# Attention in a decoder layer: row sums collected by four accumulating DMAs and used two chunks later

## What is computed

```python
qkv = jnp.einsum('bnd,ed->bne', x, w_qkv)
q, k, v = jnp.split(qkv, 3, axis=-1)          # to heads: (2, 16, 2048, 32)
dots = jnp.einsum('bhnd,bhmd->bhnm', q, k) * SCALE
attn = jax.nn.softmax(dots, axis=-1)
out = jnp.einsum('bhnm,bhmd->bhnd', attn, v)
...
x = _layernorm(x + attention)                 # then cross-attention to 77 rows, and a quantised FFN
```

## Time and profile before

| | us |
|---|---|
| median of 3 runs (lowest, highest) | 1822.68 (1819.03, 1823.56) |
| profiled execution, own time | 1825.24 |
| its span, first to last instruction | 1823.4 |
| busy TensorE, VectorE, ScalarE, GpSimd | 1770.6, 1450.9, 1445.7, 194.8 |
| mean TensorE clock granted | 0.989 of full speed |
| self-attention, first exponential to end of the last | 294.12 to about 1347.8 |

### The profile page before, as it was taken

How to read it: one execution, slowest core, us unless ns; L and a number is a source line. 1 busy time by engine, 2 the same in 40 slices (tenths; PEclk the granted TensorE clock), 3 DMA queues, 4 the chain that set the end, 5 groups by cost and what they waited for, 6 DMA issues and landing times. The chain is left out here.

```text
span 1823.4 us, 40231 instructions
## 1 busy us (share of the span) xinstructions
PE 1770.6 (97%) x15938; PEld 900.4 (49%) x15938; DVE 1450.9 (80%) x1582; ACT 1445.7 (79%) x1581; POOL 194.8 (11%) x189
## 2 busy tenths in 40 slices
PE   8999999999999999999999999999989999999997
PEld 6887885333333333333333333333346776644443
DVE  5345345988998898899998999989984778788898
ACT  5344356999999999999999999999964555555487
POOL 0000000010010010010010010010112221000044
PEclk9999999999999999999999999999999999999999
DMA  8665556658567577477566667676556340122075
GB/s 295 212 236 205 199 204 198 139 123 191 128 142 180 120 160 174 114 164 177 128 150 169 146 148 177 136 179 149 117 143 212 139 138 24 64 127 127 1 293 209
DMA packets 110832, 288.79 MB, mean 158 GB/s; under 512 B 8676, under 2 KB 25188, under 8 KB 97252
## 3 DMA queue, kind: packets, MB, share of 16 engines
q1 hardware_dynamic: 97012, 187.08, 28.7%
q0 software_dynamic: 13680, 99.62, 28.4%
HBM read 105.01 MB, written 82.05 MB: 103 GB/s over the span
## 5 line engine op out<-in xcount | busy, mean ns | idle before, releaser
L918 DVE TENSOR_TENSOR dve_sum<-dve_sum,probs 128x2048 f32<-128x2048 f32 x320 | 733.6, 2292 | 34.3 <-ACT probs L842 25.6
L842 ACT ACTIVATE probs<-score_others,shift_now 128x1536 f32<-128x1536 f32 x384 | 597.4, 1556 | 0.0
L1035 PE MATMUL mixed_ps<-probs,value_piece 128*32 128x512 f32 (+1 forms) x3840 | 402.9, 516 | 1.1 <-ACT probs L842 0.2
L841 ACT ACTIVATE probs<-score_first,shift_now 128x512 f32<-128x512 f32 x384 | 267.0, 695 | 2.2 <-PE score_others L997 1.1
L997 PE MATMUL score_first<-first_queries,key_piece 32*128 32x512 f32 x768 | 248.3, 429 | 4.3 <-ACT probs_paired L841 1.9
L997 PE MATMUL score_others<-first_queries,key_piece 32*128 32x512 f32 x2304 | 251.0, 429 | 0.0
L997 PE MATMUL score_others<-q_second,key_piece 32*128 32x512 f32 x2304 | 247.4, 424 | 0.0
L997 PE MATMUL score_first<-q_second,key_piece 32*128 32x512 f32 x768 | 245.1, 424 | 0.1
L997 PEld LDWEIGHTS score_first<-first_queries,key_piece 32*128 32x128 f32 x768 | 123.2, 185 | 186.0 <-ACT probs L841 94.9
L997 PEld LDWEIGHTS score_first<-q_second,key_piece 32*128 32x128 f32 x768 | 121.8, 183 | 183.4 <-ACT probs L841 105.4
L842 ACT ACTIVATE probs_paired<-score_others,shift_now 128x1536 f32<-128x1536 f32 x128 | 202.4, 1581 | 0.0
(11 more groups left out here) (253 smaller groups left out, 2581.7 us busy)
## 6 DMA issues: line engine op xcount, KB each, us to landing
probs_paired<-probs_paired POOLq DMA_DIRECT2D x95, 1024.0 KB, 8.4
o_scratch<-out_parts SPq DMA_DIRECT2D x33, 512.0 KB, 2.8
k_scratch<-parts SPq DMA_DIRECT2D x32, 512.0 KB, 4.6
q_scratch<-parts SPq DMA_DIRECT2D x32, 512.0 KB, 2.7
key_piece<-k_scratch SPq DMA_DIRECT2D x32, 512.0 KB, 5.1
h_scratch<-h SPq DMA_DIRECT2D x5, 2816.0 KB, 8.1
h<-h_scratch SPq DMA_DIRECT2D x5, 2816.0 KB, 11.5
v_scratch<-values SPq DMA_DIRECT2D x32, 256.0 KB, 2.0
```

The lines of the kernel that those rows point to most:

```text
L841: nc.scalar.activation(block_probs(k)[:, 0:CH], score_first[:], ACT.Exp, bias=shift[:, c:c + 1], scale=SCALE).then_inc(probs_done, 1)
L842: nc.scalar.activation(block_probs(k)[:, CH:HPG * CH], score_others[n % 2][:], ACT.Exp, bias=shift[:, c:c + 1], scale=SCALE).then_inc(prob ...
L918: nc.vector.tensor_tensor(total[:], first[:], block_probs(k)[:], ALU.add).then_inc(dve_added, 1)
L1035: last = nc.tensor.matmul(mixed_ps[j * HD:(j + 1) * HD, lo:hi], v_group[k // KPP][:, k % KPP, j * HD:(j + 1) * HD], block_probs(k)[:, j * ...
```

## The change

The pairs become late blocks, (8, 9) and (13, 14). `join_pair` adds block 9 onto 8 and 14 onto 13; `join_sum` then adds each joined pair onto `dve_sum` by a further DMA, the first after VectorE's last add of the chunk, the second after the first has landed. `dve_sum` then holds the sum of all 16 blocks, and TensorE needs one pass of sums a chunk, in step 0, on the chunk before the last one (BEHIND = 2). The results of a chunk wait in one of two buffers `mixed` meanwhile. Value products begin in step 1, with two steps of three halves instead of four. VectorE's copy of the results stands after the last add instead of before it. ScalarE waits for `pair_free` before each block of a pair, which GpSimd raises when a pair's sum has landed. SP's wait for `four_landed` goes. At the end the last two chunks' sums are made on their own: `sums_last_but_one` in step 14 of the last chunk, `sums_last` in five passes.

```diff
-    PAIRS = ((2, 3), (4, 5))
+    PAIRS = ((8, 9), (13, 14))
...
-    SUM_PARTS = 2
-    SUMS_AT = ((0,), (1,))
+    BEHIND = 2
+    CHUNKS = ITERS * CPB
...
-    VALUE_HALVES = (0, 0, 2, 2, 3, 2, 2, 3, 2, 2, 3, 2, 2, 3, 2, 2)
+    VALUE_HALVES = (0, 2, 2, 2, 2, 3, 2, 2, 2, 2, 3, 2, 2, 2, 2, 2)
...
-        mixed = sb("mixed", [P, CH], F32)
+        mixed = [sb(f"mixed{u}", [P, CH], F32) for u in range(BEHIND)]
...
-                            sp.wait_ge(four_landed, 1 + (it + 1) * CPB)
-                            values_read(0)
-                            load_v(ng, nb, 0)
-                            keys_read(2)
...
+                            for piece in range(PIECES):
+                                values_read(piece)
+                                load_v(ng, nb, piece)
+                                if piece + 2 < PIECES:
+                                    keys_read(piece + 2)
+                                    load_k(ng, nb, piece + 2)
...
-                            if i is not None and k == PAIRS[i][1]:
-                                act.wait_ge(pairs_landed, it * CPB + c + 1)
-                            elif i == 0:
-                                act.wait_ge(four_landed, it * CPB + c + 1)
-                            elif i == 1:
-                                act.wait_ge(sums_done, it * CPB + c + 2)
+                            if i is not None:
+                                act.wait_ge(pair_free, 2 * (it * CPB + c) + 1 + i)
...
+                def add(it, c, a):
+                    k = ADD_ORDER[a + 1]
+                    total = dve_sum[c % 2]
+                    v.wait_ge(probs_done, (it + 1) * EXPS + (c * KB + k + 1) * 2)
+                    if a == 0:
+
+                        v.wait_ge(sums_done, 2 + it * CPB + c)
+                        first = block_probs(ADD_ORDER[0])
+                    else:
+                        v.wait_ge(dve_added, (it * CPB + c + 1) * ADDS + a)
+                        first = total
+                    nc.vector.tensor_tensor(total[:], first[:], block_probs(k)[:], ALU.add).then_inc(dve_added, 1)
+
+                def chunk(it, c, adds):
+                    take_shift(it if c == 0 else it + 1, (c + CPB - 1) % CPB)
+                    invert(it * CPB + c)
+                    divide(it * CPB + c, c)
+                    for a in range(adds):
+                        add(it, c, a)
+
+                with v.Fori(0, ITERS - 1) as it:
                     for c in range(CPB):
...
+                        chunk(it, c, ADDS)
+                        gather(it, c + 1)
+                for c in range(CPB - 1):
+                    chunk(ITERS - 1, c, ADDS)
+                    gather(ITERS - 1, c + 1)
+                chunk(ITERS - 1, CPB - 1, ADDS - 1)
+                invert(CHUNKS, last_but_one_ps)
+                gather(ITERS - 1, CPB)
+                divide(CHUNKS, 0)
+                invert(CHUNKS + 1)
...
+                def join_pair(it, c, i):
+                    into, other = PAIRS[i]
+
+                    pool.wait_ge(mixed_done, (it + 1) * BLOCKS + c * KB + into + 1)
+                    pool.wait_ge(probs_done, (it + 1) * EXPS + (c * KB + other + 1) * 2)
+                    pool.sem_inc(may_join, 1)
+                    nc.gpsimd.dma_start(probs_paired[i][0][:], probs_paired[i][1][:], accum_op=ALU.add).then_inc(pair_joined[i], 16)
+
+                def join_sum(it, c, i):
+                    f = it * CPB + c
+                    pool.wait_ge(pair_joined[i], 16 * (f + 1))
+                    if i == 0:
+                        pool.wait_ge(dve_added, (f + 2) * ADDS)
+                    pool.sem_inc(may_join, 1)
+                    nc.gpsimd.dma_start(dve_sum[c % 2][:], probs_paired[i][0][:], accum_op=ALU.add).then_inc(sum_joined, 16)
+                    pool.wait_ge(sum_joined, 32 * f + 16 * (i + 1))
+                    pool.sem_inc(pair_free, 1)
+
                 def join(it, c):
...
+                    for i in range(len(PAIRS)):
+                        join_pair(it, c, i)
+                    for i in range(len(PAIRS)):
+                        join_sum(it, c, i)
...
+                def sums(f):
+                    pe.wait_ge(mixed_copied, f + BEHIND)
                     if f == 0:
...
+                        pe.sem_inc(sums_done, 1)
+                    elif f < BEHIND:
+                        fill().then_inc(sums_done, 1)
                     else:
...
+                        pe.wait_ge(sum_joined, 32 * (f - 1))
+                        ones_times(mixed_ps, dve_sum[f % 2], True, True).then_inc(sums_done, 1)
+
+                def sums_last_but_one():
+                    pe.wait_ge(probs_done, EXPS + (CHUNKS * KB - 1) * 2)
+                    pe.wait_ge(sum_joined, 32 * (CHUNKS - 1))
+                    ones_times(last_but_one_ps, dve_sum[CHUNKS % 2], True, True).then_inc(sums_done, 1)
+
+                def sums_last():
+                    pe.wait_ge(mixed_copied, CHUNKS + BEHIND)
+                    pe.wait_ge(probs_done, EXPS + CHUNKS * KB * 2)
+                    raw = [*PAIRS[1], ADD_ORDER[-1]]
+                    pe.wait_ge(pair_joined[0], 16 * CHUNKS)
+                    ones_times(mixed_ps, probs_paired[0][0], True, False)
+                    for k in raw:
+                        ones_times(mixed_ps, block_probs(k), False, False)
+                    pe.wait_ge(dve_added, (CHUNKS + 1) * ADDS - 1)
+                    ones_times(mixed_ps, dve_sum[(CHUNKS - 1) % 2], False, True).then_inc(sums_done, 1)
...
-                        for at in SUMS_AT[step] if step < len(SUMS_AT) else ():
-                            sums(f, at)
+                        if step == 0:
+                            sums(f)
+                        if f == CHUNKS - 1 and step == KB - AHEAD:
+                            sums_last_but_one()
```

More of the change, by code:

```diff
@@ L699, in attend @@
         dve_added, may_join = sem("dve_added"), sem("may_join")
-        pair_joined, four_joined = sem("pair_joined"), sem("four_joined")
-        pairs_landed, four_landed = sem("pairs_landed"), sem("four_landed")
+        pair_joined, sum_joined = [sem(f"pair_joined{i}") for i in range(len(PAIRS))], sem("sum_joined")
+        pair_free = sem("pair_free")
         mixed_copied = sem("mixed_copied")
@@ L815, in _ @@
                     sp.wait_ge(v_in[piece], 16 * ITERS)
-                store(ITERS, 0)
+                for c in range(BEHIND):
+                    store(ITERS, c)
             @block.scalar
@@ L896, in _ @@
                 v.wait_ge(filled, 1)
-                gather(0, 0)
-                with v.Fori(0, ITERS) as it:
-                    for c in range(CPB):
[L900 to L904, removed]
-                        for a in range(ADDS):
-                            if a == ADDS - 1:
-                                gather(it, c + 1)
-                            k = ADD_ORDER[a + 1]
-                            v.wait_ge(probs_done, (it + 1) * EXPS + (c * KB + k + 1) * 2)
-                            if a == 0:
-                                v.wait_ge(sums_done, 1 + it * CPB + c)
-                                first = block_probs(ADD_ORDER[0])
-                            else:
-                                v.wait_ge(dve_added, (it * CPB + c + 1) * ADDS + a)
-                                first = total
-                            nc.vector.tensor_tensor(total[:], first[:], block_probs(k)[:], ALU.add).then_inc(dve_added, 1)
@@ L999, in score, with ones_times @@
                     last.then_inc(scores_done, 1)
-                def sums(f, at, parts=SUM_PARTS):
-                    if at == 0:
-                        pe.wait_ge(mixed_copied, f + 1)
-                    if f == 0:
-                        if at == 0:
-                            pe.sem_inc(sums_done, 1)
-                        return
-                    if f == CHUNKS and at < len(PAIRS):
-                        part = probs_paired[at][0]
-                        pe.wait_ge(pair_joined, 16 * len(PAIRS) * CHUNKS)
-                    elif at == 0:
-                        part = probs_paired[1][0]
-                        pe.wait_ge(four_joined, 16 * f)
-                    else:
-                        part = dve_sum[(f + 1) % 2]
-                        pe.wait_ge(dve_added, (f + 1) * ADDS)
-                    for j in range(HPG):
-                        last = nc.tensor.matmul(mixed_ps[j * HD:(j + 1) * HD, :], keep.ones[:, 0:HD], part[:, j * CH:(j + 1) * CH],
-                                                start=at == 0, stop=at == parts - 1)
-                    if at == parts - 1:
-                        last.then_inc(sums_done, 1)
+                def ones_times(out, part, start, stop):
+                    for j in range(HPG):
+                        last = nc.tensor.matmul(out[j * HD:(j + 1) * HD, :], keep.ones[:, 0:HD], part[:, j * CH:(j + 1) * CH],
+                                                start=start, stop=stop)
+                    return last
```

(20 more changed lines are left out.)

64 lines of the change are left out of this document (22 added, 42 removed).

## The result

The changed kernel takes 1834.72 us (median of 5 runs, 1829.54 to 1839.56) and the kernel before 1820.06 (5 runs, 1819.03 to 1823.56): a ratio of 1.0068, 95% interval 1.0044 to 1.0092, so slower by 14.7 us where the forecast was slower by 39.6. The direction is that of the forecast and the time lies in its whole range (1805 to 1882), just under the forecast's own part of it (1836 to 1882), but the loss is less than half of what was forecast.

What follows compares the result with a forecast made beforehand. ScalarE's exponentials set the pace in two-half steps, TensorE in three-half ones. Terms -7.0 - 9.0 + 0.8 + 44.8 + 10.0 = +39.6 us on a median of 1822.7 gave 1862; range 1805 to 1882, the forecast's own 1836 to 1882.

Steps and rivals of the forecast that it cites:

- The term of -7.0: Ordinary attention chunks: two three-half TensorE steps fewer gain 0.22 us in each of 32 chunks, -7.0 us.
- Rival (c): Block 6: VectorE's first add comes too late and VectorE sets the pace, 1825 us without chain stands; chance 0.02.
- -9.0: ScalarE's four waits for POOL's joined blocks, with restarts and half-clock losses, go: -9.0 us.
- +44.8: Block 8, first chunk of an iteration: ScalarE stands 6.4 us for POOL's late accumulations, seven times, +44.8 us.
- my 9.0: POOL's chain, fourth chunk: the second sum takes 7.8 us plus 1.2 for key and value loads.
- The bound below: Lower bound of ScalarE's stand at block 8, from cheaper split and accumulations: 2.3 us, or none if loads slip into gaps.
- +10.0: TensorE after each of the seven ScalarE stands: the clock falls and loses 1.43 us each time, +10.0 us.
- +0.8: End of attention: extra inversion and five passes of last sums, less one add, +0.8 us (bounds -1.5 and +3).
- my 4.2: POOL's split of the weights, fourth chunk: takes 4.2 us amid back-to-back VectorE adds (range 3.3 to 5.7).
- Rival (b): POOL's chain is late by 1 to 3 us only, about +4 us, 1826 us; chance 0.07.
- (a): POOL's chain fits because accumulations and loads overlap more; only the gains of -15.2 us remain, 1807 us; chance 0.22.
- (d): ScalarE stands in ordinary chunks too, as an accumulation onto the sum takes 7.2 us, not 5.85: 1890 us; chance 0.05.

Runs made afterwards that it cites:

- experiment 6: Kernel of experiment 1 with four three-half steps a chunk instead of two, same 32 halves: 1810.87 us, ratio 0.9949 to the kernel before.
- experiment 7: Kernel before the change without SyncE's wait for the four joined blocks ahead of the value and key loads: 1858.86 us, ratio 1.0204.
- experiment 1: Changed kernel with GpSimd's split of the weights moved between the issues of a chunk's two pair joins: 1809.52 us, ratio 0.9947 to the kernel before.
- experiment 3: Changed kernel with the split of the weights after the sums of an iteration's first chunk instead of its third: 1807.3 us, ratio 0.9931 to the kernel before.
- experiment 5: Kernel of experiment 1 with the fourth chunk's pair (8, 9) also waiting for block 13's exponentials: 1836.14 us, ratio 1.0085 to the kernel before.
- experiment 4: Changed kernel with key piece 3 loaded to an eighth, value pieces 2 and 3 to a quarter: 1820.62 us, ratio 1.0006 to the kernel before.
- experiment 8: Changed kernel run again with nothing edited, for a second profile: 1827.97 us, ratio 1.004 to the kernel before.
- experiment 2: Changed kernel with the split of the weights moved between the pair joins in the last iteration only: 1827.52 us, ratio 1.0044 to the kernel before.

## Why the prediction was right in its mechanism and too high in its sum

**The ordinary chunk.** Right: 32.30 to 32.32 for a forecast of 32.35, two late exponentials a chunk (0.23 and 0.13). The term of -7.0 is -8.0 in the profiles. Its cause is only in part what the step said: by experiment 6 the two three-half steps fewer are 0.16 of the 0.25. What the other 0.09 is was not separated.

**The head.** Right, to 0.1 us at the transpose and the first add. Rival (c), VectorE as the pacemaker, fell: nothing waited at block 6.

**The old waits.** -9.0 was read as stands, restarts and clock, and that is what they cost: 9.1 in the four chunks of before that have them. The profiles give 11.8 for all that made chunks of before irregular; 2.3 of it is in the very first chunk, where no exponential waited for POOL. The stands at block 2 are gone. It was not tried alone; experiment 7 shows that the part of the change that merely lifts SP's wait is no gain by itself, it costs 38 us without the new order.

**POOL's chain: place and count right, size wrong.** This is the step that failed: "ScalarE stands 6.4 us, once in each of seven iterations: +44.8". The stands are where it put them, of the cause it gave (experiments 1, 3 and 5), and 13.6 us in all. Of the 4.5 us too much in each, 1.0 is the issue (+28.4 for +29.45) and 3.4 the chain from there to the release (22.1 for 25.45). That chain held 19.85 for accumulations and 5.6 for other traffic, which was added in full. Experiment 4 shows the loads at somewhat less than half of that price, 1.0 for 2.3; at the same rate the 5.6 would be about 2.4 and the chain 22.3. That the query load and the store are overcharged by the same share is argued, not tried. One term was too low: the second sum, ahead of the split, took 9.8 to 11.2 for my 9.0 (in experiment 3, where no keys or values lie beside it, 7.2 to 8.7). Key piece 2 and value piece 1, issued at +22.1 and +22.8, lie beside it and stood in no term. That the first sum had landed at +14.0 to +14.9, not at +16.25, covered this. The bound below, a stand of 2.3, was nearer than the value taken: five of the seven stands lie under it.

**The clock.** "I add the 1.43 each time, +10.0" was wrong with the stand: the clock fell after two of seven, the longest two (2.93 and 2.56), and cost 2.3 and 1.1. It did not fall after those of 1.96 or less, but in experiment 8 it did, briefly, after one of 1.89, and in the kernel before after two of the four of the earlier trace rows. The length of a short stand alone does not decide it.

**The tail.** "+0.8" missed that the late split is in the last iteration as well: the fourth pair's lateness there has no next iteration to be late in, but TensorE's last sums wait for it. It was +5.1 in the profiles; without the split in the way (experiment 1) it is 7.7 - 6.5 = +1.2, near the term.

**The lock.** The Trainium skill, "SBUF — State Buffer", section "SBUF: two separate sides", holds here: the rows of experiments 2 and 8 show GpSimd's cast held to the end of a running add. From the start of the split to the issue behind it 3.1 to 4.6 pass when the cast still gets in before the add at +25.45 (416.06 to 419.24 is 3.2) and 4.9 to 5.1 when not (416.13 to 420.99, 812.65 to 817.65), for my 4.2. What my sum lacked is that both instructions end with an add, so that the issue comes in steps of one add. My reading of the earlier trace rows was loose: the 720 ns fell not beside an idle VectorE, but beside its copy out of PSUM (397.02, 0.69), and the add behind that copy, beginning at 397.63, took 2.45 instead of 2.29.

**Against the rivals.** Rival (b), a chain late by 1 to 3 us, gave 1826 and describes the profile: 1.94 a stand for its 2, 3.4 for the clock for its 5, 1829.5. The median of the first comparison lies between it and my forecast, that of experiment 8 beside it. I gave it 0.07, for no reason but the narrowness of its interval, although my own bound below (2.3) lay inside it. (a) fell for the changed kernel, but is nearly what experiments 1 and 3 measured: 1809.5 and 1807.3 for its 1807. (d) fell: no ordinary chunk has a stand.

**What the change is worth.** With the split moved, both versions beat the kernel before (0.9947 and 0.9931) and the changed one. The change itself is worth 11 to 13 us, and an order on GpSimd's queue that it left as it was took back 17 to 25, by which comparisons one takes (1.0040 or 1.0068 against 0.9947 or 0.9931). The profiles bear this out where the edits lie, from the first exponential to the projection: 1060.2 before, 1063.5 and 1066.2 in the two profiles of the changed kernel, 1043.5 and 1045.3 in experiments 1 and 3. Why the same changed kernel has medians of 1834.7 and 1828.0 in two comparisons is not settled beyond the late casts, nor is the spread of the stages behind the projection.

## What to carry to other kernels

When accumulating DMAs begin to release buffers, look through the queue that issues them for anything that stands between one landing and the next issue: here two small elementwise instructions, moved by a few lines, were worth more than the whole change. Sum the chain with everything that lies beside each of its parts, but take a second value in which other traffic counts half (experiment 4, one case), and ask which of the two the chance belongs to; a near miss deserves as much of it as a large one. Follow a delay into the last iteration too, where it meets another consumer.

## What the runs showed of the hardware that I had not expected

- A GpSimd cast amid back-to-back VectorE adds of 2.3 us took from 0.40 to 2.50 by where its start fell against the running add, since it ends just behind that add. In the fourth chunks the DMA issued behind it went out at +28.4 or +30.7 us, two values one add apart, in executions of the same instructions.
- Plain loads beside a queue of accumulations of 1 MB cost them less than half of their own share of time (1.0 for 2.3), although two of these accumulations took 14.0 where one takes 7.3 to 8.3.
- The same load traffic let in 22 us earlier (experiment 7) cost 38 us through one accumulation in each iteration that was issued 1 to 3 us late.
